# Macaron block with strided and local attention: where the exponents' guard gets its bound

## The reference, cut to what matters

```python
x = x + 0.5 * ffn(layernorm(x))          # x is [1, 2048, 128]
x = x + attn(layernorm(x))
x = x + 0.5 * ffn(layernorm(x))

def attn(x):                              # 16 heads of 8
    q, k, v = heads(x @ q_w), heads(x @ k_w), heads(x @ v_w)
    q = q * sigmoid(unity_scale)
    scores = q @ k.T / sqrt(8)
    allowed = (j % 4 == 0) | (abs(i - j) <= 8)
    scores = where(allowed, scores, -inf)
    return (softmax(scores) @ v) @ o_w + o_b

def ffn(x):                               # 128 -> 512 -> 128
    h = gelu(butterfly(x @ W_exp + b_exp, up_weights) + up_bias)
    return butterfly(h, down_weights) @ W_con + b_con + down_bias
```

## Time and profile before

| | us |
|---|---|
| Median of 3 runs | 269.37 (268.79 to 269.7) |
| The profiled execution | 269.3 |
| Its span in the trace | 267.5 |
| TensorE busy | 249.6 (93%) |
| ScalarE busy | 196.4 (73%) |
| VectorE busy | 126.7 (47%) |
| Chain that ended last, TensorE's share | 87% |

### The profile page before, as it was taken

One profiled execution on the slowest core, in us unless ns is written; L12 is line 12 of the kernel. 1 busy time (PEld: TensorE's weight loads), 2 busy tenths in 40 slices (PEclk: granted clock), 3 DMA queues, 4 the chain that ended last, 5 costly groups with the idle time before them and its releaser, 6 DMA issues.

```text
span 267.5 us, 6937 instructions
## 1 busy us (share of the span) xinstructions
PE 249.6 (93%) x2919; PEld 138.3 (52%) x2919; DVE 126.7 (47%) x408; ACT 196.4 (73%) x256; POOL 7.3 (3%) x12
## 2 busy tenths in 40 slices
PE   1698899999789999999999999999999999899995
PEld 0482766857434344445444445434455444457775
DVE  4878357898776232035254135134235422446113
ACT  1764165576779999998899988999978999654440
POOL 9100000000000000000000000000000000000000
PEclk9999999999999999999999999999999999999999
DMA  6940000187669743411311330331230000000112
GB/s 201 269 122 9 2 1 0 56 254 208 169 169 352 245 89 80 85 57 34 87 54 32 86 84 4 87 83 36 53 86 2 0 4 2 2 0 0 42 39 78
DMA packets 23887, 21.82 MB, mean 82 GB/s; under 512 B 4743, under 2 KB 22087, under 8 KB 23835
## 3 DMA queue, kind: packets, MB, share of 16 engines
q1 hardware_dynamic: 22742, 21.02, 29.1%
q10 hardware_dynamic: 1112, 0.34, 0.6%
HBM read 13.98 MB, written 7.56 MB: 81 GB/s over the span
## 4 chain that ended last, share of the span: by engine, by line
PE 87%; ACT 5%; DVE 4%; DMA 1%; issue 1%; DVEq 0%; ACTq 0%
PE ps L670 23%; PE ps L648 22%; PE ps L494 11%; PE ps L450 9%; PE ps L655 4%; PE ps L680 4%; PE ps L464 2%; PE ps L688 2%; PE ps L700 1%; PE ps L476 1%; PE ps L437 1%; PE ps L530 1%; DMA resid<-L_attn_x 1%; PE ps L517 1%; PE ps L516 1%
## 5 line engine op out<-in xcount | busy, mean ns | idle before, releaser
L868 ACT ACTIVATE probs_all<-ps 128x1024 f32<-128x1024 f32 x128 | 122.8, 1023 | 11.1 <-PE ps L648 9.4
L670 PE MATMUL ps<-probs_all,v_strided 128*32 128x256 f32 x1024 | 68.2, 384 | 0.2 <-ACT probs_all L868 0.2
L648 PE MATMUL ps<-q_slots,k_strided 75*128 75x512 bf16 x250 | 65.3, 381 | 0.3 <-ACT probs_all L868 0.3
L670 PEld LDWEIGHTS ps<-probs_all,v_strided 128*32 128x32 f32 x1024 | 27.2, 109 | 31.8 <-issue 9.5
L1146 DVE RECIPROCAL rden<-ps 128x16 f32<-128x16 f32 x16 | 4.1, 258 | 72.1 <-PE ps L688 72.1
L648 PEld LDWEIGHTS ps<-q_slots,k_strided 75*128 75x128 bf16 x250 | 20.4, 97 | 33.6 <-issue 9.8
L450 PE MATMUL ps<-xnorm_t,up_folded 128*128 128x512 f32 x64 | 29.3, 601 | 1.7 <-ACT xnorm_t L757 1.0
L494 PE MATMUL ps<-down_folded,gelu_h 128*128 128x128 f32 x192 | 22.7, 277 | 1.2 <-ACT gelu_h L766 1.2
L766 ACT ACTIVATE gelu_h<-ps,bias_up 128x512 f32<-128x512 f32 x24 | 16.4, 687 | 10.0 <-PE ps L450 9.9
L494 PEld LDWEIGHTS ps<-down_folded,gelu_h 128*128 128x128 f32 x192 | 22.0, 192 | 2.9 <-issue 2.1
L1172 DVE SCALAR_TENSOR_TENSOR probs_all<-probs_all,mask_k_sb 128x1024 f32<-128x1024 f32 x16 | 19.6, 1223 | 3.0 <-ACT probs_all L874 2.5
(11 more groups left out here) (119 smaller groups left out, 227.5 us busy)
## 6 DMA issues: line engine op xcount, KB each, us to landing
q_slots<-q_parts SPq DMA_DIRECT2D x16, 288.0 KB
k_local<-k_local_parts SPq DMA_DIRECT2D x48, 78.0 KB
q_parts<-prologue_or_parts SPq DMA_DIRECT2D x9, 384.0 KB, 4.5
k_strided<-k_strided_parts SPq DMA_DIRECT2D x12, 96.0 KB
q_parts<-last_parts SPq DMA_DIRECT2D x3, 384.0 KB, 4.7
k_local_parts<-prologue_or_parts SPq DMA_DIRECT2D x3, 288.0 KB, 4.8
resid<-L_attn_x SPq DMA_DIRECT2D x1, 768.0 KB, 10.0
out<-resid SPq DMA_DIRECT2D x3, 256.0 KB, 2.3
```

The costliest lines, as they stand in the source:

```text
L648: mm = pe.matmul(PS[:, b0 + i, :], KS[:, ch, G * g + h, :], QS[:, g, h, :], start=True, stop=True)
L670: mm = pe.matmul(PS[VC * h:VC * (h + 1), 6 + n % 2, 0:QB // 2], VS[:, ch, at:at + VC], probs, start=(ch == 0 and r == 0), stop=False, skip ...
L868: act.activation(PE_[:, ch // 2, 2 * m:2 * m + 2, ch % 2, :], PS[:, b0:b0 + 2, :], ACT.Exp).then_inc(p_ready, 1)
```

## The change

The bound no longer comes from the queries and keys but from the weights. For each head, the largest singular values of its columns of q_w (scaled) and of k_w bound every score, since a normalized row has a squared norm of at most 128. The kernel forms the two Gram matrices, keeps the blocks of the heads, squares them twice, and takes the sum of squares of the fourth power by head, that is, the trace of the eighth. The product of both traces, scaled, must be at most 1. `SAFE` is 68 in place of 40. Steps of the guard now stand in passes 1 to 3: `gram`, `gram_squared`, `gram_fourth`, `traces`, `count_kept` on TensorE; a copy of the scaled weights, a copy and a square on ScalarE; a masked product, a sum and five short instructions on VectorE. The squares, `norm_sums` and the maxima are gone.

TensorE reads the flag in the fifth pass, behind `keep_clock`, and branches after block 3's keys and queries. The scores of the first unit are all in the attention loop. Steps 0 and 1 wait for block 3's queries and keys to be copied out, and block 3's values (TensorE's products and ScalarE's copies) follow step 2, or the second exponential. They use banks 6 and 7 in place of 5 and 6. SyncE writes block 2's keys after six of the twelve loads of local keys rather than after all of them.

```diff
 # SyncE
-            for g in range(NG):
+            for g in range(2):
                 load_k(0, g, ld_q[g])
             write_strided(2)
+            for g in range(2, NG):
+                load_k(0, g, ld_q[g])
             write_strided(NB - 1)
...
 # TensorE
+            def gram():
+                pe.wait_ge(bq_ready, 1)
+                pe.wait_ge(ld_c, 16 * 11)
+                pe.matmul(PS[:, 7, 0:P], BQ[:, :], BQ[:, :], start=True, stop=True)
+                pe.matmul(PS[:, 7, P:2 * P], KW[:, :], KW[:, :], start=True, stop=True).then_inc(bd_ps, 1)
+            def gram_squared():
+                pe.wait_ge(bd_step, 1)
+                pe.matmul(PS[:, 7, 2 * P:3 * P], BG[:, 0, :], BG[:, 0, :], start=True, stop=True)
+                pe.matmul(PS[:, 7, 3 * P:4 * P], BG[:, 1, :], BG[:, 1, :], start=True, stop=True).then_inc(bd_ps, 1)
+            def gram_fourth():
+                pe.wait_ge(bd_act, 1)
+                pe.matmul(PS[:, 7, 0:P], BG2[:, 0, :], BG2[:, 0, :], start=True, stop=True)
+                pe.matmul(PS[:, 7, P:2 * P], BG2[:, 1, :], BG2[:, 1, :], start=True, stop=True).then_inc(bd_ps, 1)
+            def traces():
+                pe.wait_ge(bd_step, 2)
+                pe.matmul(PS[:, 7, 2 * P:2 * P + 2], BM[:, 1, :], BR[:, :], start=True, stop=True).then_inc(bd_ps, 1)
+            def count_kept():
+                pe.wait_ge(one_set, 2)
+                pe.wait_ge(bd_step, 5)
+                pe.matmul(PS[0:1, 7, 0:1], BF[:, :], BO[:, :], start=True, stop=True).then_inc(bd_ps, 1)
...
                 if b == NB:
-                    skip_hint = pe.mark_branch_hint_location()
-                    norm_sums(NB - 2)
                     pe.wait_ge(y_first, 1)
                     keep_clock(0, 1)
+                    pe.wait_ge(flag_set, 1)
+                    bounded = pe.value_load(FLAG[0:1, 0:1], min_val=0, max_val=1)
                 if b:
                     turn_rows(b - 1)
+                if b == NB - 1:
+                    traces()
                 if b < NB:
                     ffn_down(b)
-                if 2 <= b < NB:
-                    norm_sums(b - 2)
...
+                if b == 1:
+                    gram()
+                if b == 2:
+                    gram_fourth()
                 if b:
                     keys_queries(b - 1)
                 if 0 < b < NB:
                     block_values(b - 1, 0, None)
+                if b == 1:
+                    gram_squared()
...
 # ScalarE, in the first unit
+                        if u == 0 and s == 2:
+                            values_out(NB - 1)
...
 # VectorE
+            def bound_product():
+                dve.wait_ge(bd_ps, 4)
+                dve.tensor_copy(BT[:, :], PS[:, 7, 2 * P:2 * P + 2]).then_inc(bd_step, 1)
+                dve.wait_ge(bd_step, 3)
+                dve.tensor_tensor(BP[:, :], BT[:, 0:1], BT[:, 1:2], ALU.mult).then_inc(bd_step, 1)
+                dve.wait_ge(bd_step, 4)
+                dve.tensor_scalar(BF[:, :], BP[:, :], 1.0, None, ALU.is_le).then_inc(bd_step, 1)
+            def bound_flag():
+                dve.wait_ge(bd_ps, 5)
+                dve.tensor_copy(BC[:, :], PS[0:1, 7, 0:1]).then_inc(bd_step, 1)
+                dve.wait_ge(bd_step, 6)
+                dve.tensor_scalar(FLAG[:, :], BC[:, :], 0.5 - P, None, ALU.is_le).then_inc(flag_set, 1)
...
                 if b < NB - 2:
                     ffn_ahead(b + 1)
...
-                if b >= 2:
-                    norms(b - 2)
+                if b == 1:
+                    dve.wait_ge(bd_ps, 1)
+                    dve.tensor_tensor(BG[:, :, :].rearrange("p a k -> p (a k)"), PS[:, 7, 0:2 * P], BM[:, :, :].rearrange("p a k -> p (a k)"),
+                                      ALU.mult).then_inc(bd_step, 1)
                 if b and b < NB - 1:
                     split_block(b - 1)
+                if b == 2:
+                    dve.wait_ge(bd_act, 2)
+                    dve.tensor_reduce(BR[:, :], BG4[:, :, :], AX.X, ALU.add).then_inc(bd_step, 1)
```

More of the change, by code:

```diff
@@ L130, in program @@
         RSN = sb("rstd_tmp", [P, NT])
-        SQ = sb("squares", [P, 2 * QB], BF16)
-        HS = sb("head_sel_sb", [P, 32], BF16)
-        NM = sb("norms", [P, NB // 2])
-        NX = sb("norms_max", [P, 1])
-        FLT = sb("bound_row", [1, 64])
-        FLP = sb("bound_products", [1, NH + 1])
+        BM = sb("head_mask_sb", [P, 2, P])
+        BQ = sb("bound_queries", [P, P])
+        BG = sb("grams", [P, 2, P])
+        BG2 = sb("grams_squared", [P, 2, P])
+        BG4 = sb("fourth_squares", [P, 2, P])
+        BR = sb("bound_sums", [P, 2])
+        BT = sb("bound_traces", [P, 2])
+        BP = sb("bound_product", [P, 1])
+        BF = sb("bound_kept", [P, 1])
+        BO = sb("minus_one", [P, 1])
+        BC = sb("bound_count", [1, 1])
         FLAG = sb("bounded", [1, 1], mybir.dt.int32)
@@ L210, in program @@
         ld_mq = sem("ld_mq")
[L211 to L214 removed]
+        bq_ready = sem("bq_ready")
+        bd_ps = sem("bd_ps")
+        bd_act = sem("bd_act")
+        bd_step = sem("bd_step")
         flag_set = sem("flag_set")
@@ L491, in ffn_down @@
                     if last and t == 2:
+                        if b < NB:
+                            count_kept()
                         pe.wait_ge(y_done, b)
@@ L533, in block_values @@
                     mm.then_inc(qkv_ps, 1)
-            def norm_sums(b):
-                pe.wait_ge(sq_done, b + 1 if b < NB - 1 else NB + 2)
-                if b >= 2:
-                    pe.wait_ge(nm_step, b - 1)
-                for c in range(2):
-                    mm = pe.matmul(PS[b % 2 * 64 + 32 * c:b % 2 * 64 + 32 * c + 32, 7, :], HS[:, :], SQ[:, QB * c:QB * (c + 1)], start=True, stop=True,
-                                   skip_group_check=True)
-                mm.then_inc(nm_ps, 1)
+            def gram():
[18 more added lines that the diff above has]
+                pe.matmul(PS[0:1, 7, 0:1], BF[:, :], BO[:, :], start=True, stop=True).then_inc(bd_ps, 1)
             def keep_clock(bank, n):
@@ L629, in _ @@
                 pe.wait_ge(ld_mq, 16 * ((PARTS + 1) * NG * NB + (PARTS + 2) * NG))
-                for k, h in ((0, 0), (0, 1), (1, 0), (1, 1), (2, 0)):
-                    first_score(k, h)
                 pe.br("pe_bounded")
             nc.switch_bb("pe_bounded")
-            pe.wait_ge(v_ready, 3 * NB)
-            first_score(2, 1).then_inc(s_ps, 3)
-            keep_clock(7, 1)
             def scores(it, g, s):
@@ L710, in _ @@
                             pe.wait_ge(ld_ks[s // 2], 16 * PARTS)
-                        if it or g or s >= 3:
-                            scores(it, g, s)
+                        if it == 0 and g == 0 and s < 2:
+                            pe.wait_ge(qk_ready, 3 * NB - 1 + s)
+                        scores(it, g, s)
+                        if it == 0 and g == 0 and s == 2:
+                            block_values(NB - 1, 0, None)
+                        if it == 0 and g == 0 and s == 3:
+                            pe.wait_ge(v_ready, 3 * NB)
                         if before and s == 1:
@@ L808, in qkv, with values_out @@
                 act.activation(lk, PS[:, 2, P:QB], ACT.Copy).then_inc(qk_ready, 1)
-                if b == NB - 2:
-                    squares(b)
+                if b < NB - 1:
+                    values_out(b)
+            def values_out(b):
                 act.wait_ge(qkv_ps, 4 * b + 4)
-                vps = (PS[:, 3:5, :] if b < NB - 1 else PS[:, 5:7, :]).rearrange("p a b -> p (a b)")
+                vps = (PS[:, 3:5, :] if b < NB - 1 else PS[:, 6:8, :]).rearrange("p a b -> p (a b)")
                 n = len(pairs_of(b))
@@ L849, in _ @@
                 if b >= 1:
-                    if 2 <= b < NB:
-                        squares(b - 2)
+                    if b == 1:
+                        act.wait_ge(sig, 3)
+                        act.wait_ge(ld_c, 16 * 11)
+                        act.activation(BQ[:, :], QW[:, :], ACT.Copy, scale=SG[:, 2:3]).then_inc(bq_ready, 1)
+                    if b == 2:
+                        act.wait_ge(bd_ps, 2)
+                        act.activation(BG2[:, :, :].rearrange("p a k -> p (a k)"), PS[:, 7, 2 * P:4 * P], ACT.Copy).then_inc(bd_act, 1)
                     qkv(b - 1)
+                    if b == 2:
+                        act.wait_ge(bd_ps, 3)
+                        act.activation(BG4[:, :, :].rearrange("p a k -> p (a k)"), PS[:, 7, 0:2 * P], ACT.Square).then_inc(bd_act, 1)
             for it in range(NB):
@@ L1022, in ffn_sum @@
                 last = b % NB == NB - 1
+                if last and b < NB:
+                    bound_product()
                 if last:
```

74 lines of the change are left out of this document (15 added, 59 removed).

## The result

| | before | after |
|---|---|---|
| Median of the runs, us | 269.53 | 277.27 |
| Lowest and highest | 268.79 to 269.84 | 274.11 to 280.25 |
| The profiled execution | 269.3 | 276.8 |
| Its span | 267.5 | 274.9 |
| Mean granted clock of TensorE in the runs | 1.000 (the profiled one) | 0.969 to 0.994 |

The changed kernel is slower, by a ratio of 1.0247 with a 95% interval of 1.0203 to 1.029. I had forecast 271.6, and 273.2 as the upper end. The direction was right, the time lies outside the range. The changed kernel's executions differ by how long TensorE's clock was low in them (274.11 us at a mean of 0.994, 277.73 at 0.975); so where the times of an experiment fall into groups, they are told with their mean granted clock, and the ratios leave out executions in a slow state (here the one of 280.25, clock 0.969).

The account below looks back on a forecast made before the run. The prediction took TensorE, with 87% of the chain, and what makes it wait as the bound. 269.3 + 4.05 + 0.37 - 2.07 = 271.65, so it forecast 271.6 us, slower; range for 8 in 10: 270.2 to 273.2.

Parts of the forecast that it names:

- Step 1 and 2: After block 1's second layer: Gram products +0.47 us, then 3.11 idle for VectorE's masked product; block 2's first layer +4.05.
- Steps 3 and 4: Passes 2 and 3: TensorE waits for VectorE's sum; block 3's second layer starts +1.47 us, ends +1.67.
- step 2: Ahead of block 2's first layer: TensorE stands still 3.11 us for the masked product, and two squares cost 0.47.
- Step 5: End of pass 3: `keep_clock` directly follows block 2's values; transposes +0.37 us, not +1.67; block 3's first key product +4.42.
- Step 6: Block 3's first key product to first values' product: 7.35 us against 9.42, so -2.07, with a branch of 0.50.
- The keys for steps 4 and 6: Keys used by those steps of the attention loop, left at nothing in the sum.
- rival A: TensorE's clock falls in the wait ahead of block 2's first layer: 2.2 us more, 273.8; chance 0.08.
- C: The branch after block 3's keys and queries costs more, its hint now in pass 2: +1.5 us, 273.1; chance 0.06.
- Rival B: Squares ahead of block 2's first layer find their operand ready: 0.94 us in place of 4.05, 268.5; chance 0.06.

Follow-up runs that it names:

- the kernel with 14 products: The changed kernel with 14 idle products of one column (56 TensorE instructions) at the program's start: 272.63 us, ratio 1.0126, in two groups.

## Why the prediction was right in its sum and wrong in its time

**Step 1 and 2, the wait: right.** Idle 3.04 for 3.11, the masked product 0.41 for 0.42. In the kernel with 14 products at full clock, block 2's first layer starts 4.08 later than before, counted from block 0's first layer in both timelines (47.80 less 21.94, against 44.21 less 22.43); I had 4.05.

**Steps 3 and 4: right.** VectorE's sum took 0.41 for 0.42; TensorE waited 1.57 ahead of `traces`, where the sum had 1.27 (61.91 less 60.64). In the kernel with 14 products at full clock block 3's second layer starts 5.41 later than before (65.56 less 21.94, against 60.64 less 22.43), of which 4.08 come from step 2: 1.33 for these two steps, where I had moved it by 1.47. `count_kept` found its operand ready, as I had said.

**Step 5: right.** `keep_clock` stands directly behind block 2's values. At full clock block 3's first key product came 4.24 late (75.19 less 21.94, against 71.44 less 22.43); I had 4.42.

**Step 6: the sentence that failed is "The branch of 0.50 fits into TensorE's wait for the queries".** I took the branch's length from a program in which the transfer of instructions next to it had begun 3.5 us ahead of it (74.33 against 77.79), and treated it as a property of the instruction. In the kernels with 0.5 us, key product to values' product takes 7.10 to 7.11 us (7.35 forecast); with 3.1 to 3.8 us and the clock full it takes 8.12 and 8.70, with 3.96 us and a clock that falls 9.95. The rest of the step was right: in the kernel with 14 products the first exponential starts 3.03 behind block 3's first key product (78.22 less 75.19), where I had put 3.1. The keys for steps 4 and 6 were no term of the sum, as I had left them; keys are late only in the kernel without the guard, whose passes end 8 us earlier than the changed kernel's.

**Step 2 failed in what it left out: the clock behind the wait stood in the sum at nothing.** So rival A happened, beside C's price. I had given A 0.08 and argued against it with a clock that read full throughout. But as I had written myself, the dense part of that trace held no gap of that length, so the row could not speak against it. And I took it as full for the prologue, where it has no record and TensorE ran at the lower level until 16.04 us. A's price of 2.2, taken from that very stretch, was small: the profiled execution lost 2.6 until block 2's second layer had ended (59.16 less 52.53 less 4.05), the two groups of the kernel with 14 products lie 3.4 apart. C's upper end for the branch was 2.0, four times 0.50, a factor that no row and no run shows; the branch took 3.96. I had priced A and C one at a time. The range of 8 in 10 reached neither A's time nor the two together.

**Rival B did not happen; its price was near.** The squares behind the layer give back 2.7 us (271.0, the lower group of the kernel with 14 products, becomes 268.25), and 3.3 in the profiled executions counted from block 0's first layer to the end of the span; I had put the stall at 3.1. Without it the change is a gain of 0.4% (ratio 0.9938 to 0.9984).

**The sum itself stands.** With the branch at 0.5 and the clock full the time was 271.0 (the lower group of one kernel) and 271.91 (all runs of another), against 271.65 for the sum; before was 269.5. Their profiled executions, 270.83 and 271.78, both come to 271.3 with block 0's first layer put where it started before (21.94 and 22.89 against 22.43). So the sum was 0.3 us too high, from its tail (7.35 for 7.10) and block 3's keys (4.42 for 4.24). What made it 277.3 were two effects that the sum had at zero. The slow branch with the fall behind it is worth 2.8 us (274.71 less 271.91, on two chips with before at 269.59 and 269.47). The fall in pass 1 is worth 2.8 by the traces: counted from block 0's first layer, block 3's first key product comes 7.03 later than before in the changed kernel (78.33 less 22.29) and 4.24 in the one with 14 products. The times give 2.1 (the profiled 276.81 less 274.71).

## What to carry to other kernels

A term read at nothing from a trace of before is only as good as the conditions under which it was read: when an edit opens a gap of some microseconds on TensorE (3.04 here), or changes how many instructions stand ahead of a branch (704 for 760), price the clock and the branch as terms (here 2.8 us each by the traces and times above) and not as rivals with a small chance, and price them together. A product that waits for another engine belongs behind work that TensorE has anyway: one layer further on, the same squares cost 0.5 us in place of 3.5 and more. Where that is not to be had, filler on TensorE kept its clock here (1.00 from 44 to 53 us, the first layer 3.60 in place of 5.91), and 20 or 56 idle instructions early in the program brought the branch to 0.49 us from 3.96. The clock's row of the page is to be checked against the distance of like products: it reads full where the trace has no record (ahead of 16.04 us in the trace of before).

## What the runs showed of the chip that I had not expected

**The branch's price depended on where it stood in the program.** With 723 to 771 of TensorE's instructions ahead of it, it took 0.41 to 0.50 us in every profile; with 704 to 716 it took 3.10 to 3.96. Other places weren't run. In the short cases the fetch of 16 KB next to it began 3.5 to 5.9 us ahead of the branch, in the long ones 0.8 to 1.6 behind its start. The hint's place made no difference in either kernel (3.82 and 3.96, 0.50 and 0.50). That it is the number of instructions ahead and nothing else in the change, the two kernels with idle products show. What sets the transfer off isn't shown: it started when TensorE had recorded 704 instructions in the kernel before, 697 with the 14 idle products and 665 with the 5, which is no fixed number, and the branch of medium length that I had expected of the last didn't come. At full clock the slow branch cost less than its own length: 1.0 and 1.6 us (8.12 and 8.70 less 7.10), as TensorE is at block 3's keys and queries for the first 2.2 us of it (78.33 to 80.51 in the changed kernel).

**One and the same gap brought the clock down in some executions and not in others.** The wait of 3.04 us in pass 1 left it full in four executions of the kernel with 14 products and went with a lower clock in the other four. A fall costs 3.4 us there. The second gap is shorter (1.96 and 1.93 us of idle time at the branch, with a wait of 0.78 for ScalarE's copy ahead of it), and the clock fell behind it too, 1.5 and 0.4 us after TensorE was at work again, once for 13.6 us; a gap of 1.82 left it full. With the quick branch and no wait of 3 us in pass 1, five of 42 executions still had a mean clock of 0.994. Why the clock falls in one execution and not in another, and why it comes back sooner, the runs don't show. They do show that its first rise, in the prologue, comes at another moment each time: at 14.99 us in the one with the gap of 3.04 and no fall, at 15.73, 17.18 and 17.36 in the three whose clock fell in it.
